# Feed-forward 0: the requantised x tile is split into fp16 halves in SBUF at the beginning of a step and transposed by DMA, no longer by TensorE

## The reference, cut to what matters

```python
def _L0_ffn_ref(X0, W0, bias0, W1, bias1):
    def _quant_dequant_fp8(x):       # per row and chunk of 128
        ...
        scale = jnp.maximum(amax, 0.0001) / 448.0
        q = (xr / scale).astype(jnp.float8_e4m3fn)
        return (q.astype(jnp.float32) * scale).reshape(M, K)
    ...
    D = Xd @ W0d.T + bias0           # (tokens x 512) @ (512 x 1792), Xd quantised and dequantised
    D = jax.nn.gelu(D, approximate=False)
    D = D.astype(compute_dtype).astype(jnp.float32)
    Dd = _quant_dequant_fp8(D)
    E = Dd @ W1d.T + bias1           # (tokens x 1792) @ (1792 x 512)
    return E.astype(compute_dtype).reshape(B, L, H)
...
x = x + _L0_ffn_ref(_layernorm(x, axis=-1), L0_ffn_W0, L0_ffn_bias0, L0_ffn_W1, L0_ffn_bias1)
```

## Time and profile before

| | |
|---|---|
| time of a run, median of 3 | 1792.19 us (1788.71 to 1792.46) |
| the profiled execution | 1791.77 us, its span 1790.1 us |
| feed-forward 0 in the trace | from about 1022 to 1397 us after the span's start |
| busy over the span | PE 89%, DVE 74%, ACT 44%, POOL 17% |
| mean granted TensorE clock | 0.959 of full speed |

### The profile page before, as it was taken

One profiled execution on the slowest core, in us unless ns is written; L12 is line 12 of the kernel. 1 busy time (PEld: TensorE's weight loads), 2 busy tenths in 40 slices (PEclk: granted clock), 3 DMA queues, 4 the chain that ended last, 5 costly groups with the idle time before them and its releaser, 6 DMA issues. The chain is left out here.

```text
span 1790.1 us, 29876 instructions
## 1 busy us (share of the span) xinstructions
PE 1595.8 (89%) x11014; PEld 864.1 (48%) x11014; DVE 1318.4 (74%) x2481; ACT 779.5 (44%) x1646; POOL 306.1 (17%) x244
## 2 busy tenths in 40 slices
PE   4899999999999999999999568899997796888786
PEld 3455555555555555555555234445443354555443
DVE  6567667776676676767768579899998436999687
ACT  3424243334242434342424155667675323555442
POOL 2001000010010000100000101111210224777510
PEclk9899999999999999999999889999998898999888
DMA  6022312212222213132203111223224101000002
GB/s 247 21 75 44 87 50 58 71 48 72 71 48 83 60 48 75 44 77 66 68 17 106 58 52 27 42 44 59 41 43 89 31 1 36 0 0 0 1 1 94
DMA packets 206239, 96.49 MB, mean 54 GB/s; under 512 B 171570, under 2 KB 187955, under 8 KB 205876
## 3 DMA queue, kind: packets, MB, share of 16 engines
q1 hardware_dynamic: 167236, 61.89, 14.3%
q10 hardware_dynamic: 38896, 33.03, 5.8%
HBM read 44.57 MB, written 11.53 MB: 31 GB/s over the span
## 5 line engine op out<-in xcount | busy, mean ns | idle before, releaser
L528 PE MATMUL pj<-XT,WQ 128*128 128x512 f16 x1536 | 338.4, 380 | 6.5 <-PEq L330 6.5
L570 PE MATMUL xp<-WO,OT 128*128 128x512 f16 x1536 | 338.3, 380 | 1.8 <-DVE X L801 1.8
L570 PEld LDWEIGHTS xp<-WO,OT 128*128 128x128 f16 x1536 | 147.7, 98 | 183.6 <-issue 11.4
L528 PEld LDWEIGHTS pj<-XT,WQ 128*128 128x128 f16 x1536 | 148.4, 98 | 181.7 <-DVE WKV L294 6.7
L645 ACT ACTIVATE E<-E 128x512 f32<-128x512 f32 x64 | 40.2, 627 | 345.3 <-DVE E L739 345.3
L801 DVE SCALAR_TENSOR_TENSOR X<-xp,X 128x512 f32<-128x512 f32 x128 | 88.1, 690 | 119.1 <-PE xp L570 118.0
L508 POOL TENSOR_TENSOR VW<-VW,XB 128x1024 f32<-128x1024 f32 x14 | 33.0, 2355 | 769.3 <-DVE VW L107 769.3
L922 PE MATMUL db<-W0T,XD 128*128 128x448 f16 x768 | 162.3, 363 | 0.0
L939 PE MATMUL eb<-W1T,DT 128*128 128x512 f16 x672 | 151.2, 385 | 3.0 <-DMA DT<-HL 3.0
L704 DVE SCALAR_TENSOR_TENSOR QT<-pj,QT 128x512 f16<-128x512 f32 x128 | 88.0, 687 | 67.5 <-ACT QT L628 67.2
L922 PEld LDWEIGHTS db<-W0T,XD 128*128 128x128 f16 x768 | 77.2, 101 | 74.6 <-issue 8.6
(11 more groups left out here) (226 smaller groups left out, 2659.1 us busy)
## 6 DMA issues: line engine op xcount, KB each, us to landing
W0T<-in_L_xattn_wq ACTq DMA_DIRECT2D x7, 1024.0 KB, 5.5
W0T<-in_L_xattn_wo ACTq DMA_DIRECT2D x7, 1024.0 KB, 5.1
CS<-in_ctx SPq DMA_DIRECT2D x4, 1024.0 KB, 10.0
X<-in_x SPq DMA_DIRECT2D x4, 1024.0 KB, 11.1
out<-X SPq DMA_DIRECT2D x8, 512.0 KB, 3.6
XB<-in_L_ffn_W ACTq DMA_DIRECT2D x28, 128.0 KB, 2.7
w0t<-XB ACTq DMA_DIRECT2D x7, 512.0 KB, 3.3
w1t<-W0T ACTq DMA_DIRECT2D x7, 512.0 KB, 3.8
```

The costliest lines, as they stand in the source:

```text
L528: last = pe.matmul(bank[:, :], w, src[:, b, k, tokens], start=n == 0, stop=n == 3 * KC - 1)
L570: last = pe.matmul(xp[i % 2][:, :], OT[:, a, j, i * P:(i + 1) * P], WO[:, b, j, :], start=n == 0, stop=n == 3 * REP - 1)
```

## The change

Before, TensorE transposes the float tile and the split follows behind it, out of PSUM. After, the split comes first, into a new SBUF buffer `XHL` (one buffer, not two), and SP issues two DMA transposes of it, into `XD`. The cast `high_x` and the subtraction `low_x` move to the first place of the step on ACT and DVE, ahead of `out_e` and `grid_d`. The transposes in SP's queue stand ahead of those of the hidden tile. PE waits for them before the first product, and `XHL` is only written again once its last transposes have landed.

```diff
+        XHL = sb(ph, "XHL", [P, 2, KC, P], F16)
...
-        xt = pb(ph, "xt")
...
         # SP
             def step(i):
-                hidden = ahead(i, -1)
+                hidden, nxt = ahead(i, -1), ahead(i, 1)
+                if live(nxt):
+                    if live(ahead(nxt, -2)):
+                        sp.wait_ge(S["d_done"], count(nxt, 4, -4))
+                    for half, split in enumerate(("xh_done", "xl_done")):
+                        sp.wait_ge(S[split], count(nxt, 1, 1))
+                        sp.dma_start_transpose(XD[:, nxt[1] % 2, half, :, :],
+                                               XHL[:, half, :, :].rearrange("p k t -> p (k t)")).then_inc(S["xt_done"], 16)
...
-            for i in range(TILES + 1):
+            for i in range(-1, TILES + 1):
...
         # PE
-                        pe.wait_ge(S["xt_lo"], count(i, 1, 1))
+                        pe.wait_ge(S["xt_done"], count(i, 32, 32))
...
-            def transpose_x(i):
-                pe.wait_ge(S["xqs_done"], count(i, 1, 1))
-                for k in range(KC):
-                    last = pe.transpose(xt[:, k * P:(k + 1) * P], QX[:, k, :], ident[:, :])
-                last.then_inc(S["xt_done"], 1)
...
-                if live(nxt):
-                    transpose_x(nxt)
...
         # ACT
             def high_x(i):
-                act.wait_ge(S["xt_done"], count(i, 1, 1))
-                act.activation(XD[:, i[1] % 2, 0, :, :], xt[:, :].rearrange("p (k t) -> p k t", k=KC), ACT.Copy).then_inc(S["xt_hi"], 1)
+                if live(ahead(i, -1)):
+                    act.wait_ge(S["xt_done"], count(i, 32, 0))
+                act.wait_ge(S["xqs_done"], count(i, 1, 1))
+                act.activation(XHL[:, 0, :, :], QX[:, :, :], ACT.Copy).then_inc(S["xh_done"], 1)
 
             def step(i):
                 older, hidden, nxt, after = (ahead(i, by) for by in (-3, -1, 1, 2))
+                if live(nxt):
+                    high_x(nxt)
                 if live(older):
                     out_e(older)
...
                     gelu(i, (3,))
-                if live(nxt):
-                    high_x(nxt)
...
         # DVE
             def low_x(i):
-                dve.wait_ge(S["xt_hi"], count(i, 1, 1))
-                dve.tensor_tensor(XD[:, i[1] % 2, 1, :, :], xt[:, :].rearrange("p (k t) -> p k t", k=KC), XD[:, i[1] % 2, 0, :, :],
-                                  ALU.subtract).then_inc(S["xt_lo"], 1)
+                if live(ahead(i, -1)):
+                    dve.wait_ge(S["xt_done"], count(i, 32, 0))
+                dve.wait_ge(S["xh_done"], count(i, 1, 1))
+                dve.tensor_tensor(XHL[:, 1, :, :], QX[:, :, :], XHL[:, 0, :, :], ALU.subtract).then_inc(S["xl_done"], 1)
...
             def step(i):
                 hidden, nxt, after = (ahead(i, by) for by in (-1, 1, 2))
+                if live(nxt):
+                    low_x(nxt)
                 if live(hidden):
                     grid_d(hidden)
...
                     amax_d(i, 1)
-                if live(nxt):
-                    low_x(nxt)
                 if live(i):
                     scales_d(i)
...
         # POOL, before QX is written again
-                    pool.wait_ge(S["xt_done"], count(i, 1, 0))
+                    pool.wait_ge(S["xl_done"], count(i, 1, 0))
```

More of the change, by code:

```diff
@@ L851, in ffn0 @@
         db = [pb(ph, f"db{i}") for i in range(4)]
-        xt = pb(ph, "xt")
         eb = pb(ph, "eb")
         names = ("w1_ld b_ld "
-                 "xt_done xt_hi xt_lo d_done ones_done bias_zeroed bias_ready gelu_done da_done dstep dw_done dcut dbits dm_done dsum "
+                 "xt_done xh_done xl_done d_done ones_done bias_zeroed bias_ready gelu_done da_done dstep dw_done dcut dbits dm_done dsum "
                  "dq_done dqs_done dh_done dl_done dt_done e_done eb_done x_done")
@@ L943, in step @@
             def step(i):
-                old, nxt = ahead(i, -2), ahead(i, 1)
+                old = ahead(i, -2)
                 if fixed(i) == 0:
```

## The result

The changed kernel takes 1820.6 us (median of 4 runs, 1819.2 to 1821.3) against 1790.9 before: slower, ratio 1.0164, 95% interval 1.0152 to 1.0177. The forecast was 1820, the range 1812 to 1828. The profiled execution has a span of 1817.5 us, 27.4 more than the one before.

The account below looks back on a forecast made before the run. DVE's queue was taken to set the pace. Boundaries cost 29.7 us, 9.0 came back mid-step, net 20.7; the first tile's 7.1 made 27.8, which on 1791.8 gave 1820 us, range 1812 to 1828.

Parts of the forecast that it names:

- DVE sets the pace, PE's transposes are worth nothing: Feed-forward steps: DVE's queue sets the 19.47 us step, so removing 7 us of PE's transposes gains nothing.
- low_x in front of grid_d: Step boundary: low_x waits 2.8 us for ACT's cast; L100 starts 5.6 after L85, not 2.40; 8 x 3.2 = 25.6 us.
- x pieces cover the first six boundaries: Ahead of steps 1 to 6 an x piece covers ACT's time; only 1.1 more at step 5, 3.0 at the others.
- The steady steps: Ahead of steps 7 to 14: boundary 3.2 us longer, 0.60 back mid-step; step 19.47 + 2.6 = 22.1 us.
- The first tile: Block start: the first transposes move after W1T's bytes in SP's queue, so PE starts 7.1 us later; bounds 0.1 to 9.8.
- The row of wq: Evidence for queue order: wq's 1 MB load, behind four 1 MB loads on SP's queue, needs 13.6 us, Wq's 6.3.
- The DMA transposes in steady state: Steady steps: new transposes land 2.9 us after issue, have 7 us of slack and cost nothing.
- The sum of 1829: Case of a tile's eight blocks transposed one after another, 10.5 us: first tile costs 16 us, total 1829.
- What I said of PE's wait: Steady steps: PE idles 3.1 us in each, before the second product, waiting for DT.
- rival B: PE slows to a lower clock after waits and takes the pace, up to 1869; 2.0 of 3.1 us stays hidden; chance 0.04.
- The end: Behind step 14 no x is left; boundaries and last products stay as before, nothing changes.
- The sum: 20.7 for the steps + 7.1 for the start = 27.8, on the profiled 1791.8: 1819.6, so 1820 for a run.

Follow-up runs that it names:

- e8: e1 with QX in two buffers, so POOL need not wait for low_x before writing the next tile; 1800.0 us, ratio 1.0036 to the kernel before.
- e4: Changed kernel with only ACT's cast high_x moved ahead of the 14 multiplications, not behind them; 1795.9 us, ratio 1.0025 to the kernel before.
- e10: Changed kernel with ACT's cast in the middle of its 14 multiplications, behind 7 of them; 1802.5 us, ratio 1.0052 to the kernel before.
- e2: Changed kernel with W1T's load issued on SP's queue behind the first x tile's two transposes; 1814.5 us, ratio 1.0122 to the kernel before.
- e3: Changed kernel with W1T's load issued by ACT at the block's start, on another queue; 1820.4 us, ratio 1.0156 to the kernel before.
- e9: Changed kernel with W1T's load in two halves, one ahead of the first x transposes, one behind; 1817.9 us, ratio 1.0139 to the kernel before.
- e1: Changed kernel with high_x and low_x back in the middle of the step, SBUF split and DMA transposes kept; 1818.1 us, ratio 1.0139 to the kernel before.
- e7: Changed kernel with the edits of e4 and e2 together; 1790.0 us, ratio 0.9983 to the kernel before.

## Why the prediction was right, step by step

*DVE sets the pace, PE's transposes are worth nothing.* Right. PE lost the 7 us of its transposes and the block grew; in e8, with that work gone and no stall, the step is what it was.

*low_x in front of grid_d.* Right in mechanism and size. L100 was forecast 5.6 after L85 and is at 5.56 to 5.71, the stall 2.8 and is 2.78 to 2.85, the step 22.1 and is 22.01. So the 0.60 in the middle of the step did come back too: the boundary grew by 3.2 and the step by 2.54. e4 and e10 show that the work ahead of the cast makes it.

*x pieces cover the first six boundaries.* Nearly. From the start of ACT's multiplications for tile 0 (1051.68 after, 1046.09 before) to those for tile 6 (1194.82, 1187.52) the block lost 1.7 us, where the terms give 4.1 - 6 x 0.60 = 0.5. The excess of 1.2 is spread over the steps (0.1 to 0.2 in most, 0.4 in the last); what makes it stays open.

*The steady steps.* From tile 6 to tile 14 (1369.08 after, 1341.25 before) the loss is 27.83 - 7.30 = 20.5 us; the terms give 8 x 2.6 = 20.8.

*The first tile.* The size was nearly right, 7.1 forecast and 6.5 measured, and W1T is the cause (e2). Two terms of the sum were off and partly cancel: W1T landed 11.1 us after its issue and not 12.7, and the last transpose 1.1 behind it and not 0.2. The step of the argument that failed is that the transposes wait because they stand behind W1T in SP's queue: with W1T on another queue they are as late (e3). The row of wq, which I took as evidence of queue order, shows as well what e9 shows, a transfer behind many bytes. The Trainium skill (DMA: Bandwidth & Descriptors, Issuing engines are not separate DMA queues) says that DMAs of all issuing engines end up on the same 16 DMA engines. That page's point was the nearer one, though it speaks of them as interleaved, and a sharing by bytes is not what e3's high half looks like, which took 11.1 us in place of 2.5. Turns by packets, as worked out above, would fit it; that is not tested.

*The DMA transposes in steady state.* Right: they land 2.5 us after issue (2.9 forecast), and even with them in the middle of the step, e8, nothing is lost. The sum of 1829, with eight blocks one after another, did not come true. The Trainium skill (VectorE: DVE Perf Modes, The three transpose paths) gives its 1309 ns for one block; no run here has a single block, and four of them landed in 2.5 us.

*What I said of PE's wait* was half right. It was forecast at 3.1 us a step, ended by DT. In the steady steps it is 2.1 to 2.8 or 0.45, ended by EB, ACT's L1004, which the cast now pushes behind it, and DT follows 0.3 to 0.4 us later. I had not counted that L936 waits for EB. The price of the lower clock in rival B, 2.0 us and hidden, is 1.7 in three of the eight steps (10.93 and not 9.24), and hidden by the same stall.

*The end.* Forecast: nothing. In the pair of profiles the last second product takes longer:

```profile
1411.61 0.61 PE L936 MATMUL eb<-B1S,ones 128*128 128x512 bf16 x1 [7.79 <-ACT EB L1004]
...
1412.01 12.00 PE L940 MATMUL eb<-W1T,DT 128*128 128x512 f16 x42
```

Before it was 10.84. With the same order of work it is 10.35 in e2, 10.41 in e3 and 11.96 in e9, so the difference of 1.2 can't be put down to the change. The parts outside the block came out 2.3 us shorter in this execution than in the one before (0.7 ahead of it, 1.6 behind), which no edit explains; with them the block's 29.7 make the span's 27.4. The medians differ by 29.7.

*The sum.* The block's 29.7 are, with the forecast in brackets, 6.3 up to the first tile's multiplications (7.1 for the start less one `low_x`, 6.5), 1.7 up to tile 6 (0.5), 20.5 up to tile 14 (20.8) and 1.2 at the end (0). The change was forecast at 27.8 and is 29.7 by the medians. That the time itself, 1820, is met to 0.6 us has luck in it: the sum was put on 1791.8, and the kernel before has since had a median of 1790.9.

## What to carry to other kernels

When a pair "cast on one engine, subtraction on the other" is moved, look at what stands ahead of the first half in its engine's queue: the second half inherits that wait, and everything behind it too. A 0.6 us instruction behind 4.2 us of ACT's work cost 2.5 us a step as the full DVE waited for it, and nothing when put into ACT's own idle time. Hold back a big load until a stage's first small DMAs are issued; putting it on the other queue did not help here; and when a buffer is read later than before, ask which engine writes it next and beside whom it will then run.

## What the runs showed of the hardware

A POOL operation on 128x512 stretched a DVE instruction on 128x14 from 0.17 to 0.99 us (L72) and 1.08 us (L73), each until POOL's ended, while L70 and L71, just before POOL began, took 0.17. Beside the large subtraction the price is smaller for DVE, 2.93 instead of 2.08 us for the pair, and POOL's own two take 1.71 and 2.00 instead of 1.04 and 1.15. The Trainium skill (SBUF — State Buffer, Who interferes with whom) describes, for the port pair that DVE and GpSimd share, an exclusive lock that blocks the loser fully; e1's rows agree with it.

A load of 3.5 MB on ACT's queue delayed a transpose of 128x512 fp16 on SP's queue from 2.5 to 11.1 us, and even the bias loads there (DVE waited 5.47 us for them in e3; before 2.45 us, and for POOL).

Behind the long idle times at the block's end PE's 42 matmuls of a second product ran in part at the lower clock (1.2 GHz), and for how long did not go by the wait. They took 9.23 us at a granted clock of 1.00, 10.35 (e2) and 10.37 (e7) at a mean of 0.89 behind waits of 8.2 and 7.8 us, 10.84 (before) at 0.84 behind 6.2, and 12.00 (after) at 0.77 behind 7.8. In the changed kernel's steady steps waits of 2.1 to 2.2 us were followed by 10.93 three times and by 9.24 once.
